# Position tables of the second and third head group: eight 128-column jobs in the second layer's stage instead of four and four 64-column jobs in two stages

## What is computed

```
rel_h = jnp.einsum('bhwc,hkc->bhwk', r_q, Rh)
rel_w = jnp.einsum('bhwc,wkc->bhwk', r_q, Rw)
attn_bias = (rel_h[:, :, :, :, None] + rel_w[:, :, :, None, :]).reshape(Bx * NUM_HEADS, S, S)
scores = q @ jnp.swapaxes(k, -1, -2) * SCALE + attn_bias
attn = jax.nn.softmax(scores, axis=-1)
```

## Time and profile before

| | us |
|---|---|
| median of 3 runs | 4869.27 (4869.14 to 4873.89) |
| the profiled execution, its own time | 4862.39 |
| its span, first to last instruction | 4860.6 |
| one turn of the loop, 1009.45 to 1300.03 | 290.58 |
| main0 in it | 157.13 |
| main1 in it | 74.60 |

### The profile page before, as it was taken

How to read it: one execution, slowest core, us unless ns; L and a number is a source line. 1 busy time by engine, 2 the same in 40 slices (tenths; PEclk the granted TensorE clock), 3 DMA queues, 4 the chain that set the end, 5 groups by cost and what they waited for, 6 DMA issues and landing times.

```text
span 4860.6 us, 97545 instructions
## 1 busy us (share of the span) xinstructions
PE 4446.6 (91%) x32598; PEld 2268.6 (47%) x32598; DVE 3079.8 (63%) x5558; ACT 2594.1 (53%) x3955; POOL 892.4 (18%) x1901
## 2 busy tenths in 40 slices
PE   4879999999999999999999999999999999999988
PEld 3334453544535454453544535454453544535434
DVE  3736667666675756657566675756757566675644
ACT  1533556555564655555555565555546555565564
POOL 4122021222202222021222202222031221202111
PEclk7988999999999999999999999999999999999999
DMA  6333152442514433153442424433253432424402
GB/s 123 87 73 77 44 119 64 100 87 56 107 42 107 88 89 75 44 115 68 100 80 58 101 52 103 91 83 75 45 114 75 100 80 49 103 60 100 88 15 40
DMA packets 235869, 386.05 MB, mean 79 GB/s; under 512 B 58396, under 2 KB 133728, under 8 KB 235360
## 3 DMA queue, kind: packets, MB, share of 16 engines
q1 hardware_dynamic: 189280, 266.13, 23.7%
q10 hardware_dynamic: 21504, 75.51, 7.8%
q0 software_dynamic: 24576, 37.80, 4.9%
HBM read 227.79 MB, written 88.08 MB: 65 GB/s over the span
## 4 chain that ended last, share of the span: by engine, by line
PE 71%; DVE 11%; issue 6%; DMA 5%; SPq 5%; ACT 2%; DVEq 0%; ACTq 0%; POOL 0%
PE P L1143 14%; PE P L1161 13%; PE P L1102 12%; DVE mx L909 7%; PE P L966 5%; PE P L967 5%; PE P L1193 4%; PE P L1214 4%; DMA queries<-oraw 4%; PE P L1110 3%; PE P L1079 3%; SPq L514 3%; DVE mxc L915 2%; PE P L1186 1%; PE P L1231 1%
## 5 line engine op out<-in xcount | busy, mean ns | idle before, releaser
L909 DVE TENSOR_REDUCE mx<-P 128x1 f32<-128x512 f32 x3072 | 1921.3, 684 | 457.4 <-PE P L1102 453.3
L779 ACT ACTIVATE probs<-P 128x1024 f32<-128x1024 f32 x1536 | 1507.5, 1022 | 854.0 <-PE P L1161 853.8
L1102 PE MATMUL P<-K,AR 96*128 96x256 f16 x6144 | 1074.1, 278 | 56.6 <-DMA AR<-biases 29.5
L1161 PE MATMUL P<-AR,K 113*128 113x512 f16 x3072 | 924.9, 383 | 13.2 <-DMA AR<-mrow 12.6
L915 DVE TENSOR_REDUCE mxc<-P 128x1 f32<-128x336 f32 (+1 forms) x1536 | 656.3, 474 | 317.9 <-PE P L1111 315.0
L1143 PE MATMUL P<-probs,V 128*17 128x512 f32 x6144 | 813.5, 601 | 5.7 <-ACT probs L779 5.7
L1102 PEld LDWEIGHTS P<-K,AR 96*128 96x128 f16 x6144 | 532.2, 98 | 581.4 <-DVE mx L909 202.0
L795 ACT ACTIVATE probs<-P 128x320 f32<-128x320 f32 (+3 forms) x1632 | 612.1, 437 | 338.2 <-PE P L1214 268.4
L1161 PEld LDWEIGHTS P<-AR,K 113*128 113x128 f16 x3072 | 213.3, 98 | 670.3 <-ACT probs L779 519.6
L1110 PE MATMUL P<-K,A 112*128 112x320 f16 (+1 forms) x1536 | 405.2, 300 | 68.7 <-DVE mx L909 54.9
L1214 PE MATMUL P<-A,K 113*128 113x320 f16 (+2 forms) x1536 | 428.3, 300 | 14.7 <-ACT probs L795 14.3
(11 more groups left out here) (125 smaller groups left out, 3718.4 us busy)
## 6 DMA issues: line engine op xcount, KB each, us to landing
AR<-biases SPq DMA_DIRECT2D x384, 256.0 KB, 7.9
AR<-queries ACTq DMA_DIRECT2D x96, 512.0 KB, 5.9
biases<-xn SPq DMA_DIRECT2D x128, 256.0 KB, 2.6
AR<-queries ACTq DMA_DIRECT2D x96, 256.0 KB, 8.8
K<-oraw POOLq DMA_DIRECT2D x384, 64.0 KB, 4.7
xin<-in_x_dram SPq DMA_DIRECT2D x16, 768.0 KB, 10.5
queries<-oraw SPq DMA_DIRECT2D x384, 32.0 KB, 4.6
QA<-queries SPq DMA_DIRECT2D x192, 64.0 KB, 2.8
```

Of the source, the lines that this page charges most:

```text
L779: nc.scalar.activation(probs[:, u % RING, j:j + 2, :], P[:, b:b + 2, :], ACT.Exp).then_inc(p_done[0], 1)
L909: V_.reduce_max(mx[:, n // 2, n % 2:n % 2 + 1], bank, AX.X).then_inc(used, 1)
L1102: last = mm(bank[:, QD * (v % 2):QD * (v % 2) + QD], AR[0:ROWS_MAX[0], part % SLOTS, v, c, j, 128 * q:128 * q + 128], K0[0:ROWS_MAX[0], h, ...
L1161: last = mm(P[:, j, :], K0[0:ROWS, h, 128 * kt:128 * kt + 128], AR[0:ROWS, p % SLOTS, kt // 2, :, j, :], start=True, stop=True)
```

## The change

Sets 1 and 2 are made together, in main1 of the turn before: eight rel jobs with eight heads each, at steps 9, 11, ... 23. A job has 8 products of 128 columns in place of 16 of 64; jobs 0 to 3 are table 0, jobs 4 to 7 are table 1. main0 has no rel jobs any more. `QA` gets three places, and SyncE loads the blocks of sets 1 and 2 right behind each other. The finished pair of sets stands in the three thirds of `oraw` and in the first 1024 columns of `xin`; it is taken away in two lots of four transfers, after job 3 and after job 7. ScalarE waits at the first job of the pair that the old contents of `oraw` have been moved (`rows_moved`), and before its first output into `oraw` that all of the pair has left (`rel_moved`). Three waits go: TensorE's for set 2 in main0 and for the row of ones in out of layer 0, and GpSimd's before that row.

```
-RELS = 4
+RELS = 4, 8
...
-    placed += [(8 + 3 * n, job) for n, job in enumerate(rel_jobs(image, 2))]
...
-    placed += [(8 + 2 * n, job) for n, job in enumerate(rel_jobs(n0, 1))]
+    placed += [(9 + 2 * n, job) for n, job in enumerate(rel_jobs(n0, 1))]
...
-        QA = sb("QA", [128, 2, GH, QD], F16)
-        rest = sb("rest", [128, GH * QD], F16)
+        QA = sb("QA", [128, G, GH, QD], F16)
+        pairs = [flat[:, n * S:n * S + S] for n in range(G)] + [xin[:].rearrange("p t c -> p (t c)")[:, 0:S]]
...
+        relhi, rello = [tables[0:2], pairs[0:4:2]], [tables[2:4], pairs[1:4:2]]
...
-            def biases_away(im, g):
-
+            def biases_away(im, part, n):
+
+                lines = 32 // RELS[part]
                 for s, (t, ready) in enumerate(((relhi, relhi_done), (rello, rello_done))):
-                    sp.wait_ge(ready, (im * G + g + 1) * RELS)
-                    for table in range(2):
-                        sp.dma_start(biases[g, table, :, s].rearrange("k a h n -> k a (h n)"),
-                                     t[g][table]).then_inc(biases_out[g], 16)
+                    sp.wait_ge(ready, im * sum(RELS) + part * RELS[0] + n + 1)
+                    for table in (range(2) if part == 0 else [n * lines // 16]):
+                        for k in range(part + 1):
+                            sp.dma_start(biases[part + k, table, :, s].rearrange("k a h n -> k a (h n)"),
+                                         t[part][table][:, GH * k:GH * k + GH, :]
+                                         ).then_inc(biases_out[part + k], 16)
...
                 query_blocks(im, 1)
+                query_blocks(im, 2)
...
                     fill_slot(image, part)
-                    if part == 2:
-                        query_blocks(image, 2)
...
-                if what == "rel" and n == RELS - 1:
-                    biases_away(image, part)
+                if what == "rel" and n in (3, 7):
+                    biases_away(image, part, n)
...
+            def rel_moved():
+
+                while staged:
+                    image = staged.pop()
+                    for g in (1, 2):
+                        act.wait_ge(biases_out[g], (image + 1) * PER_BIASES)
...
                     if job[0] == "rel":
+                        if job[3] and job[4] == 0:
+                            rows_moved()
+                            staged.append(job[2])
...
             def local_out(im, g, half):

                 rows_moved()
+                rel_moved()
...
-                    q = QA[:, part % 2, :, :].rearrange("p h (l w) -> p h l w", w=16)
-                    table = n // 2
-                    for b in range(8):
-                        line = 8 * (n % 2) + b
+                    q = QA[:, sets[0]:sets[1], :, :].rearrange("p g h (l w) -> p (g h) l w", w=16)
+                    table, cols = n * lines // 16, 512 // lines
+                    for b in range(lines):
+                        line = n * lines % 16 + b
                         rhs = q[:, :, :, line] if table else q[:, :, line, :]
                         for s in range(2):
                             lhs = Z[:, table, s, 15 - line:47 - line, :].rearrange("p x a -> p (x a)")
-                            last = mm(bank[:, 64 * b:64 * b + 64], lhs, rhs, start=(s == 0), stop=(s == 1))
+                            last = mm(bank[:, cols * b:cols * b + cols], lhs, rhs, start=(s == 0), stop=(s == 1))
...
-                    if u == 2 * TT - 1:
-                        pe.wait_ge(biases_out[2], (im + 1) * PER_BIASES)
```

More of the change, by code:

```diff
@@ L81, in rel_jobs @@
 def rel_jobs(image, g):
-    return [("rel", 0, image, g, n) for n in range(RELS)]
+    return [("rel", 0, image, g, n) for n in range(RELS[g])]
 def stat_jobs(layer, image):
@@ L259, in attention_kernel @@
         Z = sb("Z", [128, 2, 2, 48, 4], F16)
-        QA = sb("QA", [128, 2, GH, QD], F16)
-        rest = sb("rest", [128, GH * QD], F16)
-        spare = xin[:].rearrange("p t c -> p (t c)").bitcast(F16)
+        QA = sb("QA", [128, G, GH, QD], F16)
+        pairs = [flat[:, n * S:n * S + S] for n in range(G)] + [xin[:].rearrange("p t c -> p (t c)")[:, 0:S]]
+        pairs = [t.bitcast(F16).rearrange("p (m q) -> p m q", q=QD) for t in pairs]
         tables = [xn[:, n, :].bitcast(F16)[:, k * S:(k + 1) * S] for n in range(2) for k in range(2)]
-        others = [spare[:, k * S:(k + 1) * S] for k in range(3)] + [rest[:]]
-        relhi, rello = ([[t.rearrange("p (h q) -> p h q", h=GH) for t in (s[2 * n:2 * n + 2])]
-                         for s in (tables, others, tables)] for n in range(2))
+        tables = [t.rearrange("p (m q) -> p m q", q=QD) for t in tables]
+        relhi, rello = [tables[0:2], pairs[0:4:2]], [tables[2:4], pairs[1:4:2]]
         xsum = sb("xsum", [128, 2, C])
@@ L321, in attention_kernel @@
         ar_in = [sem(f"ar_in{p}") for p in range(PHASES[0])]
-        ones_done, ones_again = sems("ones_done"), sem("ones_again")
+        ones_done, ones_again = sem("ones_done"), sem("ones_again")
         mid_out, mid_in = sem("mid_out"), sem("mid_in")
@@ L386, in consumed @@
             if kind == "rel":
-                return rello_done, (image * G + part) * RELS + n + 1
+                return rello_done, image * sum(RELS) + part * RELS[0] + n + 1
             if kind == "stat":
@@ L390, in consumed, with rel_view @@
             return smax_used[layer], image * PER_ITEMS[layer] + part * (ITEMS[layer] + 1) + n + 1
-        def rel_view(bank, n, operand):
-            table, part = n // 2, 8 * (n % 2)
-            t = operand[table].rearrange("p h (l w) -> p h l w", w=16)
+        def rel_view(bank, n, operand, part):
+            lines, heads = 32 // RELS[part], GH * (part + 1)
+            table, first = n * lines // 16, n * lines % 16
+            t = operand[part][table].rearrange("p m (l w) -> p m l w", w=16)
             if table == 0:
-                return bank.rearrange("p (l h w) -> p h l w", l=8, h=GH), t[:, :, part:part + 8, :]
-            return bank.rearrange("p (w h l) -> p h l w", w=8, h=GH), t[:, :, :, part:part + 8]
+                return bank.rearrange("p (l m w) -> p m l w", l=lines, m=heads), t[:, :, first:first + lines, :]
+            return bank.rearrange("p (w m l) -> p m l w", w=lines, m=heads), t[:, :, :, first:first + lines]
         def rows_to_operands(queue, L, im, part, copies, done, take_wait=None):
@@ L477, in query_blocks @@
                 for a in range(4):
[L478 removed]
+                    sp.dma_start(QA[32 * a:32 * a + 32, g, :, :],
                                  queries[g, :, :, a, :, :].rearrange("s d h n -> (s d) h n")).then_inc(qa_in[g], 16)
[L481 removed]
+            def biases_away(im, part, n):
+                lines = 32 // RELS[part]
                 for s, (t, ready) in enumerate(((relhi, relhi_done), (rello, rello_done))):
[L484 to L487 removed]
+                    sp.wait_ge(ready, im * sum(RELS) + part * RELS[0] + n + 1)
[4 more added lines that the diff above has]
+                                         ).then_inc(biases_out[part + k], 16)
             def fill_slot(im, p):
@@ L552, in stage @@
                         sp.wait_ge(out_in, im * 16)
+                    if is_image(im, 0) or is_image(im, 1):
+                        for g in (1, 2):
+                            sp.wait_ge(biases_out[g], (im + 1) * PER_BIASES)
                     sp.dma_start(xin[:], x_t[im + 1]).then_inc(xin_in, 16)
@@ L573, in stage @@
                         sp.wait_ge(mid_out, stored)
+                        if not (isinstance(im, int) and im + 2 >= B):
+                            sp.wait_ge(biases_out[1], (im + 3) * PER_BIASES)
+                            sp.wait_ge(biases_out[2], (im + 3) * PER_BIASES)
                         sp.dma_start(xin[:], mid[im]).then_inc(mid_in, 16)
@@ L705, in stage @@
                 again = kind == "jobs" and any(job[0] == "rel" for e in after for _, job, _ in e)
-                if again or kind == "out" and (L == 0 or not (isinstance(im, int) and im + 2 >= B)):
-                    g, image = (0, im) if again else (2, im) if L == 0 else (0, im + 2)
-                    pool.wait_ge(biases_out[g], (image + 1) * PER_BIASES)
+                if again or kind == "out" and L == 1 and not (isinstance(im, int) and im + 2 >= B):
+                    image = im if again else im + 2
+                    pool.wait_ge(biases_out[0], (image + 1) * PER_BIASES)
                     take_wait()
-                    done, count = (ones_again, im + 1) if again else (ones_done[L], im + 1)
+                    done, count = (ones_again if again else ones_done), im + 1
                     nc.gpsimd.memset(xn[CH:CH + 1, 1, :], 1.0).then_inc(done, 1)
@@ L736, in _ @@
                     copy(dst, P[0:CH, t % 4, 0:GC], D ** -0.5 if m // G == 1 else 1.0).then_inc(wt_done, 1)
-            prepared = []
+            prepared, staged = [], []
+            def rel_moved():
+                while staged:
```

(25 more changed lines are left out.)

## The result

| | before | changed |
|---|---|---|
| median of 4 runs each, us | 4869.2 (4866.74 to 4873.89) | 4934.29 (4920.15 to 4936.04) |
| ratio | | 1.0136, 95% interval 1.0119 to 1.0152 |
| span of the profiled execution | 4860.6 | 4931.2 |

The change costs 65 us, 1.4%; forecast were 95 us more in a range of 31 to 136. In a second comparison the same kernel was 1.0153 (1.0139 to 1.0167) of the kernel before.

A forecast was written before the change was run, and what follows sets the result against it. TensorE, busy 91% of the span, was taken as the bound. Main0 -69, main1 +155 (+11.1 over 14 turns) and the jobs stages +9 gave +95 us on the 4869.3 us median: 4964 us, range 4900 to 5005.

The forecast's parts named there:

- The price per column: Table 1 products on TensorE: 1.83 ns per column for values 32 bytes apart, so wider products save nothing by themselves.
- the other end: Table 1 products on TensorE: cost per product, 117 ns, the same figure as the median weight load.
- main0: Four jobs leave each of 16 such stages: -4.3 us each, bounds -5.4 and -3.2, together -69 us.
- The arrival: Query blocks at the first job in main1: TensorE starts 1.9 us later, as set 2 is needed too.
- The work: Main1 holds eight jobs in place of four: +4.7 us of TensorE a turn.
- the waits between the jobs: Main1: TensorE reaches jobs 1 and 4 of the pair before their banks are free, +1.1 us, bounds 0 and 2.5.
- ScalarE's wait: Main1, before the first output into `oraw`: waiting until the pair has left costs +1.8 us, bounds 0 and 4.
- The clock: Main1: falls to half clock behind the query wait and partly in slow jobs, +1.6 us, bounds 0 and 3.5.
- The jobs stages: Two stages that make a set more of columns at one go: +4.5 us each, +9 us.
- A: Rival: extra columns are paid, but ScalarE's wait and the clock cost nothing; 4917 us, chance 0.20.
- B: Rival: the slow price is per product, so the kernel becomes faster, 4841 us, or 4904 with all waits; chance 0.11.
- C: Rival: the waits bite fully, ScalarE's at 4 us and the clock at 3.4; 5020 us, chance 0.09.

The follow-up runs named there:

- split64: Changed kernel with each product of 128 columns made as two of 64; 4944.22 us, later 4956.1 us beside 4944.2 us for the changed kernel.
- packed_after: Changed kernel with table 1 products reading the queries as table 0 does, so its column tables hold wrong values; 4916.55 us, ratio 1.0104 to the kernel before.
- packed_before: Kernel before the change with table 1 products reading the queries as table 0 does (wrong column tables); 4800.07 us, ratio 0.9868.
- turned: Changed kernel with VectorE copying the queries once into packed order in main1, results whole; 4935.37 us, ratio 1.0132 to the kernel before.
- turned_narrow: turned, with ScalarE's first output of main1 waiting for the first lot of the pair alone; 4842.39 us, ratio 0.9946 to the kernel before.

## Why the prediction was right, and where it was not

**The price per column** held. 128 columns 32 bytes apart took 230 ns a product, 16 values in a row 58 ns; the other end, 117 ns a product, is refuted by the trace, by split64 and by packed_after together. What is new is that widening may still give 10 us.

**main0: -69 us forecast, -97 measured.** The term of the sum was mis-sized: -6.1 us a main0 and not -4.3. I gave back half a microsecond for VectorE's reductions. The row of TensorE's waits in main0, which answers the earlier trace rows, hardly rose:

```profile
PE P L1128 <- DVE mx L928: 3.9, 12, 0.4
```

And this one of the main0 before, for a rel job's subtraction, is gone after:

```profile
PE P L1102 <- DVE xn L896: 0.7, 1, 0.7
```

The undisturbed main0 fell from 157.13 to 151.93, 5.2 us: the 4.7 of work and such waits of the rel jobs, so the bound of -5.4 was the nearer one. Most of the other 0.9 goes with the clock: before, five main0 of 14 took 158.6 to 160.2 us with a granted clock of 0.98 to 0.99; after, all 14 take 151.9. I had no term for that. packed_before shows how much of it is the stride: there the mean main0 is 155.5.

**The arrival: 1.9 us forecast, 1.9 measured** (14.1 to 16.0 us after the start of main1), from the landing of the last store and four more loads. TensorE's own wait there was 4.1 us on the mean where 4.5 was forecast. **The work, 4.7 us,** and **the waits between the jobs** (1.1 forecast; 0.83 at the first slow job, against the timeline above, and nothing of note elsewhere) are in the rest of 61.5 to 71.1.

**ScalarE's wait: 1.8 us forecast, 0 measured.** This step failed in the changed kernel, though the mechanism is there. Counted from the start of main1, the forecast put ScalarE through with step 29 at 37.1 us (1232) and the pair away at 39.1 to 40.6 (1234 to 1235.5). In the turn shown the pair was away at 40.8, little later than forecast, but ScalarE was ready only at 40.9 (1239.98), 3.8 us later than forecast, since the clock had slowed the steps behind the arrival and again those from 24 on. In packed_after and turned, which have no slow jobs in main1, ScalarE stands 5.2 us on the mean. The terms for this wait and for the clock were not independent, and I added them.

**The clock: 1.6 us forecast, about 4 in the runs**, not measured by itself but the remainder of 11.5 - 1.9 - 4.7 - 0.8. I expected one fall behind the wait and perhaps a second one in the slow jobs; both came, and the second lasts 10 to 14 us in 13 of the 14 turns. The two errors, 1.8 too much and 2.5 too little, nearly cancel, and main1 came out at 11.5 where 11.1 was forecast. That the sum is so close is luck in these two terms.

**The jobs stages: +9 forecast, +6 measured.** The stage of image 1 rose from 105.1 to 110.9 us; that of image 0 stood for transfers anyway.

Against the 70.6 us between the two spans the sum was 24 too high: main0 makes 28 of it and the jobs stages 3, and main1 takes 6 back. Of the rivals, A was right on ScalarE's wait and wrong on the clock, and its 4917 us lies nearer to the measured 4934 than the forecast of 4964 does. B is refuted, C's 5020 was far off.

## What to carry to other kernels

Before moving products, look at what one costs per column in each read pattern: four table 1 jobs were 80% of the time of the eight, and no width changes that, while one copy into packed order does. A wait that is covered by slow work is not gone; it comes back in full when the work gets fast, so take both away together and ask of each buffer how little of it the next writer needs. Several waits that lie at the same place are not to be added up.

## What the runs showed of the hardware

A product whose moving values stand 32 bytes apart ran at 1.8 ns a column against 0.46 ns packed at full clock. The slow ones ran the same at either clock level (2.05 us a job at full and 2.08 at half clock).

Slow jobs were followed by half clock just as waits were. From 1222.77, where the first slow job of the pair starts, to 1229.25 TensorE was busy all 6.48 us at full clock, and there the third stretch begins. This fall starts 26 to 33 us after the start of main1 in each of the 14 turns. packed_after has none in this place; its second one comes 36 to 39 us after the start of main1, inside ScalarE's wait or at its end. turned_narrow, which has neither the slow jobs nor that wait, has none from 15 to 75 us. What it is in the slow jobs that brings the clock down, no run separates. The slow jobs cost nothing at half clock, the dense ones behind them do: from step 26 to the end main1 took 47.2 us before and 49.4 in the changed kernel, with the same work in it.
